# A macaron block on one core: who widens the digit columns and scales the first norm's tiles, and when x is issued

## What is computed

```python
x = x + 0.5 * ffn(layernorm(x))
x = x + attn(layernorm(x), w_qkv, w_out)        # 16 heads of 16, causal, 4096 tokens
x = x + 0.5 * ffn(layernorm(x))

def layernorm(x): return (x - mean(x)) / sqrt(var(x) + 1e-5)
def ffn(x):                                     # 8 experts, 3 layers, top 2
    logits = x @ gate_w + gate_b
    probs = softmax(logits, axis=1)             # over the tokens
    vals, idx = top_k(probs, 2)                 # over the experts
    ... three relu layers per expert; tokens summed per expert with their weights;
    each token gets the sum of its two experts' vectors
```

## Time and profile before

| what | value |
|---|---|
| median of 3 runs | 2264.23 us (2263.72 to 2271.89) |
| the profiled execution, whole time | 2265.92 us |
| the profiled execution, span from first to last instruction | 2264.2 us |
| TensorE busy | 2152.1 us, 95% of the span |
| VectorE busy | 1855.9 us, 82% |
| ScalarE busy | 1612.2 us, 71% |
| GpSimd busy | 533.9 us, 24% |
| mean granted TensorE clock | 0.973 |

### The profile page before, as it was taken

How to read it: one execution, slowest core, us unless ns; L and a number is a source line. 1 busy time by engine, 2 the same in 40 slices (tenths; PEclk the granted TensorE clock), 3 DMA queues, 4 the chain that set the end, 5 groups by cost and what they waited for, 6 DMA issues and landing times.

```text
span 2264.2 us, 98001 instructions
## 1 busy us (share of the span) xinstructions
PE 2152.1 (95%) x42449; PEld 1871.4 (83%) x42449; DVE 1855.9 (82%) x3881; ACT 1612.2 (71%) x3536; POOL 533.9 (24%) x1311
## 2 busy tenths in 40 slices
PE   4799989999999999999999999999999999789997
PEld 2688866389999999999999899998999997568885
DVE  6655556699999999999999999999999993765555
ACT  2344445488888888888888888888888887334442
POOL 2333302421221221312212212122122211033330
PEclk9799989999999999999999999999999999879998
DMA  6411102410010100101101001010010002141112
GB/s 205 120 44 49 47 8 91 154 38 11 25 29 7 32 23 13 32 7 29 27 9 32 16 20 32 4 32 25 11 32 11 25 4 86 30 120 46 47 47 81
DMA packets 95527, 96.23 MB, mean 43 GB/s; under 512 B 41332, under 2 KB 84088, under 8 KB 95096
## 3 DMA queue, kind: packets, MB, share of 16 engines
q0 software_dynamic: 42048, 44.80, 7.9%
q1 hardware_dynamic: 52624, 45.15, 6.3%
q10 hardware_dynamic: 424, 0.01, 0.0%
HBM read 64.14 MB, written 25.43 MB: 40 GB/s over the span
## 4 chain that ended last, share of the span: by engine, by line
PE 89%; DVE 4%; issue 3%; ACT 1%; POOL 1%; DMA 1%; SPq 1%; ACTq 0%; POOLq 0%; DVEq 0%
PE bank L1090 43%; PE bank L1082 19%; PE bank L991 18%; PE bank L1128 2%; PE bank L1002 1%; PE bank L1045 1%; PE bank L1193 1%; PE bank L971 1%; DVE rows L1241 1%; DVE stats L1223 1%; PE bank L1009 1%; PE bank L1136 1%; PE bank L1058 0%; SPq L624 0%; DVE x_res L1492 0%
## 5 line engine op out<-in xcount | busy, mean ns | idle before, releaser
L1090 PE MATMUL bank<-work 96*32 96x512 bf16 (+4 forms) x17920 | 1411.9, 362 | 2.8 <-DVE work L1531 2.3
L830 ACT ACTIVATE feat<-bank 128x512 f32<-128x512 f32 (+3 forms) x2304 | 1251.3, 565 | 152.2 <-PE bank L1090 75.3
L1531 DVE TENSOR_REDUCE work<-bank 128x1 f32<-128x512 f32 (+3 forms) x2176 | 1298.4, 639 | 62.1 <-PE bank L1090 50.3
L1082 PE MATMUL bank<-feat,phase 128*17 128x128 f32 x16896 | 1138.1, 272 | 2.4 <-issue 2.4
L1082 PEld LDWEIGHTS bank<-feat,phase 128*17 128x17 f32 x16896 | 829.5, 98 | 67.8 <-issue 3.1
L1090 PEld LDWEIGHTS bank<-work 96*32 96x32 bf16 (+1 forms) x17920 | 807.3, 96 | 68.0 <-DVE work L1531 11.1
L991 PE MATMUL bank<-work 128*128 128x256 f32 x1872 | 435.1, 382 | 3.6 <-issue 2.0
L991 PEld LDWEIGHTS bank<-work 128*128 128x128 f32 x1872 | 340.7, 191 | 53.9 <-issue 12.3
L1429 DVE COPY work<-phase 128x514 f32 x234 | 100.5, 430 | 190.6 <-ACT work L779 60.7
L563 POOL TENSOR_SCALAR_AFFINE_SELECT feat<-feat 128x128 f32<-128x128 f32 x512 | 146.6, 294 | 442.5 <-ACT feat L830 435.9
L505 POOL DMA_INDIRECT work<-token_table,row_no x156 | 149.8, 961 | 327.7 <-DVE work L1443 243.6
(11 more groups left out here) (173 smaller groups left out, 1417.1 us busy)
## 6 DMA issues: line engine op xcount, KB each, us to landing
phase<-in_w SPq DMA_DIRECT2D x12, 1024.0 KB, 12.3
work<-qk_parts POOLq DMA_DIRECT2D x60, 192.0 KB, 4.2
token_table<-rows SPq DMA_DIRECT2D x8, 1056.0 KB, 9.6
qk_parts<-phase SPq DMA_DIRECT2D x20, 384.0 KB, 2.7
work<-qk_parts POOLq DMA_DIRECT2D x60, 128.0 KB, 4.3
qk_parts<-work SPq DMA_DIRECT2D x12, 384.0 KB, 2.6
x_res<-in_x SPq DMA_DIRECT2D x8, 512.0 KB, 6.5
work<-work SPq DMA_DIRECT2D x256, 1.0 KB
```

The lines of the kernel that those rows point to most:

```text
L830: eng.activation(p_ring[:, n % P_RING, lo:QB], s_bank("probs", n)[:, lo:QB], ACT.Exp, scale=HD ** -0.5).then_inc(sig.s_done, 1)
L1082: mm = eng.matmul(bank[ACC_BANK][GRID * g:GRID * g + VW, 0:P], v_aug[:, t, h, :], p_ring[:, n % P_RING, g * P:(g + 1) * P], start=(t == 0) ...
L1090: mm = eng.matmul(out[GRID * g:GRID * (g + 1), width], left[:, GRID * g:GRID * (g + 1)], right, start=start, stop=stop)
L1531: eng.tensor_reduce(maxima[:, h % 2, j, i, k + 1:k + 2], scores[:, 0:hi - lo], AX_X, ALU.max).then_inc(sig.a_done, 1)
```

## The change

Four edits:
1. SyncE's wait ahead of the second x transfer goes.
2. The two copies that widen the digit rows go from GpSimd to ScalarE, behind the exponential and ahead of the widening of the chosen experts. For the second feed-forward their wait for attention's last product moves with them, and two waits that ScalarE had just behind now stand ahead.
3. In the first norm, ScalarE makes the last two tiles of each group of four (`BY_SCALAR`), as rstd * x + shift, in one instruction each. VectorE makes shift = -mean * rstd for the four tiles (a new SCALAR_TENSOR_TENSOR on four columns) and normalises only the first two tiles.
4. ScalarE's order in the first norm: square root of group m + 1, its two tiles of group m, then the copies of group m - 1 and the gate's copy of group m - 2. TensorE's order stays; its transposes wait for two counters instead of one.

```diff
@@ GpSimd, route(f)
-                if f == 1:
-                    need.wait_ge(sig.pv, PV_ALL)
-                else:
-                    after()
-                eng.tensor_copy(lo_wide, bc(lo_ids[:, :], 2, [P, P, HOTS])).then_inc(sig.ids[f], 1)
-                eng.tensor_copy(hi_wide, bc(hi_ids[:, :], 2, [P, N_SUB, HOTS])).then_inc(sig.ids[f], 1)
                 need.wait_ge(sig.routed[f], ROUTED["col_max"])
@@ SyncE
                 a, b = g * LN_GRP[0], (g + 1) * LN_GRP[0]
-                if g == 1:
-
-                    need.wait_ge(sig.const, ident_at[0])
                 eng.dma_start(x_res[:, a:b, :], x_rows[:, a:b, :]).then_inc(sig.x_loaded[g], 16)
@@ ScalarE
+            def widen_ids(f):
+                if f == 0:
+                    need.wait_ge(sig.const, n_const[0])
+                else:
+                    need.wait_ge(sig.pv, PV_ALL)
+                    need.wait_ge(sig.s_full, S_ALL)
+                    need.wait_ge(sig.divided, len(UNITS))
+                eng.activation(lo_wide, bc(lo_ids[:, :], 2, [P, P, HOTS]), ACT.Copy).then_inc(sig.ids[f], 1)
+                eng.activation(hi_wide, bc(hi_ids[:, :], 2, [P, N_SUB, HOTS]), ACT.Copy).then_inc(sig.ids[f], 1)
+
             def first_norm():
                 sqrt_of(0, 0)
                 for m in range(GATES):
                     if m + 1 < GATES:
                         sqrt_of(0, m + 1)
-                    copy_feat(0, m)
+                    need.wait_ge(sig.shift, m + 1)
+                    for i in range((m + 1) * LN_GRP[0] - BY_SCALAR, (m + 1) * LN_GRP[0]):
+                        eng.activation(rows[:, i, 0:D], x_res[:, i, :], ACT.Identity, scale=rstd[:, 0, i:i + 1],
+                                       bias=rstd[:, 2, i:i + 1]).then_inc(sig.normed_s, 1)
                     if m:
-                        copy_gate(0, m - 1)
+                        copy_feat(0, m - 1)
+                    if m > 1:
+                        copy_gate(0, m - 2)
+                copy_feat(0, GATES - 1)
+                copy_gate(0, GATES - 2)
                 copy_gate(0, GATES - 1)
@@ ScalarE, route(f)
                 eng.activation(probs[:, :, :], logits[:, :, :], ACT.Exp).then_inc(sig.gexp[f], 1)
+                widen_ids(f)
                 need.wait_ge(sig.routed[f], ROUTED["chosen"])
@@ TensorE, transpose_rows
-                            need.wait_ge(sig.normed[n], i + 1)
+                            by_vector = LN_GRP[0] - BY_SCALAR
+                            if n:
+                                need.wait_ge(sig.normed[n], i + 1)
+                            elif i - i0 < by_vector:
+                                need.wait_ge(sig.normed[0], g * by_vector + i - i0 + 1)
+                            else:
+                                need.wait_ge(sig.normed_s, g * BY_SCALAR + i - i0 - by_vector + 1)
@@ VectorE, normalise
                 need.wait_ge(sig.rstd[n], g + 1)
+                if n == 0:
+                    eng.scalar_tensor_tensor(rstd[:, 2, a:b], mean_var[:, a:b, 0], -1.0, rstd[:, 0, a:b], ALU.mult,
+                                             ALU.mult).then_inc(sig.shift, 1)
+                    b -= BY_SCALAR
```

More of the change, by code:

```diff
@@ L44 @@
 LN_GRP = (4, 4, GRP)
+BY_SCALAR = 2
 COMBINE_GRP = (LN_GRP[1], GRP)
@@ L222, in __init__ @@
         self.sqrt, self.rstd, self.normed = many("sqrt", 3), many("rstd", 3), many("normed", 3)
+        self.shift, self.normed_s = one("mean_times_rstd"), one("normed_by_scalar")
         self.tr, self.feat = many("transposed", 3), many("feat_copied", 3)
@@ L276, in macaron_block @@
         mean_var = sb("mean_var", [P, NT, 2])
-        rstd = sb("rstd", [P, 2, NT])
+        rstd = sb("rstd", [P, 3, NT])
         w_qkv_sb = sb("w_qkv_sb", [P, KD, 3 * D])
```

## The result

The changed kernel takes 2256.22 us (median, 2252.56 to 2270.34) where the kernel before takes 2265.15 us (2262.28 to 2271.89) on the same chip. The ratio is 0.9959, 95% interval 0.9951 to 0.9967: 9.3 us less, with an interval of 7.5 to 11.1. The forecast was 11.1 us less. That is at the edge of the interval, so the sum was about right and somewhat too large. The median lies 3.1 us over the forecast's 2253.1; 0.9 of that is the kernel before, which takes 2265.15 us here and 2264.23 in the runs that the forecast counted from. It is inside the whole range (to 2260.0) and outside the sum's own range (2251.7 to 2254.8); 9.3 us less than 2264.2 would be 2254.9, just outside it too. A change within 0.5% was the likeliest of the three outcomes and is what came. The profiled execution takes 2256.6 us with a span of 2254.6, 9.6 less than the span before, at the same mean clock of 0.973.

What follows compares the result with a forecast made beforehand. VectorE's work before routing was taken as the bound at the head. Gains 5.85 + 2.40 + 4.72 less 1.9 give 11.1 us, so 2264.2 becomes 2253.1 us; range 2249.8 to 2260.0.

Steps and rivals of the forecast that it cites:

- the sum's own range: Whole time 2251.7 to 2254.8 us around 2253.1, from later x, the short instruction, ScalarE's tiles and better overlap.
- What bounds the kernel: Program head: the chain runs through VectorE until routing begins at 45.82 us; bringing routing forward brings everything behind it forward.
- The x wait, 5.85: Second x transfer no longer waits for the identity: 6.15 us VectorE idle less 0.3 for a later first transfer.
- The wide copies, 2.40: First norm: without GpSimd's wide copies beside them, VectorE's four tiles take 1.38 us instead of 3.78.
- The split norm on VectorE, 4.72: First norm: VectorE's group takes 2.84 us instead of 3.43, over eight groups.
- The end of the norm, -1.9: ScalarE's queue at the norm's end makes the tail behind VectorE 5.8 us instead of 3.9.
- TensorE: Norm transposes: slow at 3.4 us a group for three or four groups, then some 2.1, unseen by the chain.
- rival (b): TensorE stays at the low rate through the norm: routing near 40.4, gain 5.4 us, time 2258.8; chance 0.08.
- Rival (d): Expert layers: the clock rises eight matmuls earlier or later, 1.7 us either way; 0.10 beyond the forecast's range.
- Widening on ScalarE, 3 us hidden with 4.4 to spare: Both feed-forwards: the wide copies take about 3 us in ScalarE's idle time behind the exponential and cost nothing.
- Rival (a): GpSimd's code load slowed by x traffic: identity at 13.8, all-reduce 4.4 us late, time 2257.5; chance 0.15.
- Rival (c): GpSimd's code load starves: identity near 38 us, routing at 60, 14 us late, time 2278; chance 0.05.

Runs made afterwards that it cites:

- copies_only: The kernel before with only the two wide widening copies moved from GpSimd to ScalarE; routing begins at 43.22 us, whole-time ratio 0.9984 (0.9974 to 0.9993).
- x_and_copies: The changed kernel without the split norm: x wait gone and wide copies on ScalarE; routing begins at 38.32 us, ratio 0.9967 (0.9955 to 0.998).
- late_identity: The changed kernel with a 4096-column GpSimd fill ahead of the identity; routing begins at 35.79 us, ratio 0.9959 (0.9943 to 0.9974).

## Why the prediction was right, and where it was off

- **What bounds the kernel.** Right. Everything behind the start of routing moved with it by 8.8 to 11.3 us, and the routing chain kept its 19.8 us.
- **The x wait, 5.85.** Alone it brings 6.51. That is 6.15 less 0.77 for the later first transfer (I took 0.3, the range went to 1.2), and 1.1 more because the wide copies then stall VectorE for less. The start of some 1.3 us in that range stands in no row of the prediction; from issue to first packet the trace of the kernel before has 1.04 us (9.94 to 10.98) for the second transfer and 1.68 (0.80 to 2.48) for the first.
- **The wide copies, 2.40.** Here the attribution failed, not the sum. The number was read correctly from the earlier trace rows and comes back in `copies_only` (2.60, the second x being 0.25 us earlier besides). But it belongs to the place where the copies fell in the kernel before. With x early they begin beside statistics, which they don't stop, and cost 1.22 to 1.26. I added a stall to an edit that shifts it. That the smaller constants leave no mark was true of that trace only: the fill of `zeros_bf` costs 0.3 to 0.5 us wherever it falls beside tiles.
- **The split norm on VectorE, 4.72.** Right: 2.85 a step against 2.84.
- **The end of the norm, -1.9.** Right in kind, 2.2 in size. The pair of tiles is the term that was too small: 1.09 us for two, the next instruction starting 1.00 us after they began, and I took 0.75 from the 0.42 of the earlier trace rows. That row is an activation of the same 256 elements without a scale or a bias from SBUF; with both, as here, it is 0.5 us from one to the next.
- **TensorE.** Right: three slow groups, then fast, and rival (b) didn't happen. Rival (d) is seen in small, 0.45 us of its 1.7, as a gain.
- **Widening on ScalarE, 3 us hidden with 4.4 to spare.** Right: 1.89 + 1.23, with 4.51 and 4.44 left.
- **Rival (a).** Its mechanism is real and my reason against it was wrong; its price at these sizes is at most 0.2 us. It was priced as if a late identity reached TensorE's last group. **Rival (c)** asked for an identity later than 23 us; it came at 11.5 and 12.8.

So the two terms of the sum that were mis-sized are the late first x (0.77 instead of 0.3) and the tail (2.2 instead of 1.9, by ScalarE's pair of tiles). With both put right, 11.1 becomes 10.3, where 10.23 was measured at routing. The copies' term is too large by itself and the x wait's too small by the same amount, and in the changed kernel no stall is left, so the two together hold: 6.15 - 0.77 + 2.40 = 7.78 against 7.50 in `x_and_copies`, where the fill of `zeros_bf` takes back 0.37. That the fill costs nothing in the changed kernel, and that the two errors cancel, the prediction didn't know; so far the closeness of the sum is luck. The other 0.9 us between 10.2 at routing and 9.3 in the whole time is within the interval of the whole time, and the runs assign it to nothing.

## What to carry to other kernels

- Cost a stall between two engines by which instructions fall beside each other, and say so for the timing after the change; when one edit shifts the time and another removes the stall, only their joint price is readable from the trace, and each alone is worth something else.
- A late start of an engine with slack behind it is free until that slack is used up; price it through the engine that catches up, not one for one. Conversely an order that works one step behind has a tail of one more step: count it at the end of the loop.
- Where a gain of a few microseconds ends at one identifiable instruction, compare that instruction's start; the whole time carries the scatter of stages that the edit doesn't touch.

## What the runs showed of the hardware

- Beside a bf16 copy of 2048 or 1248 columns on GpSimd, VectorE's BN_STATS keep their 1.40 us for four, while TensorScalar and ScalarTensorTensor instructions, even on four columns, end only with the copy: 0.67, 0.49 and 1.05 us instead of 0.17 and 0.16, and two tiles 3.35 instead of 0.73. A GpSimd fill of 128x512 bf16 (0.52 to 0.58 us) does it too: four tiles 1.67 instead of 1.38, two tiles 1.13 and 1.18 instead of 0.73.
- The idle time ahead of GpSimd's first affine select is 7.2 us without x traffic, 8.2 to 8.6 where x pauses behind its first group, and 10.2 to 12.0 with all of it queued, with packets of x and of the small loads only in the changed kernel's first 12 us.
- The first of eight queued 512 KB transfers lands about 0.8 us later than when it is alone (6.49 to 6.57 against 5.64 to 5.72; once 7.51), though it is first in its queue.
- ScalarE takes 1.09 us for two 128x256 tiles with scale and bias per partition; from PSUM, a copy of 512 columns takes 0.60, two 1.06.
- TensorE's slow pace ends 12.5 us after the norm's first transpose before (16.59 to 29.07), 8.5 in the changed kernel (11.82 to 20.30) and 4.0 in `late_identity` (15.07 to 19.04), where it had sixteen transposes to do without a gap.
